# Attention scores of a decoder layer: six bf16 partial products, or three float32r ones in two halves of the array

## The reference, cut to what matters

```python
q = jnp.einsum('oc,bct->bot', Wq, target) + bq[None, :, None]
k = jnp.einsum('oc,bcs->bos', Wk, source) + bk[None, :, None]
v = jnp.einsum('oc,bcs->bos', Wv, source) + bv[None, :, None]
...
dot = jnp.einsum('bhdt,bhds->bhts', q, k) / math.sqrt(HEAD_DIM)
mask = target_mask[:, :, :, None] * source_mask[:, :, None, :]
dot = mask * dot - (1.0 - mask) * NEG
amap = jax.nn.softmax(dot, axis=-1) * mask
out = jnp.einsum('bhts,bhds->bhdt', amap, v)
```

## Time and profile before

| | before |
|---|---|
| median of three runs | 3174.01 us |
| runs | 3170.85 to 3174.55 us |
| span of the profiled execution | 3175.0 us |
| PE, busy | 2991.9 us (94%) |
| DVE, busy | 2833.2 us (89%) |
| ACT, busy | 2419.9 us (76%) |
| POOL, busy | 2094.4 us (66%) |
| bytes moved by DMA | 312.0 MB |

### The profile page before, as it was taken

The page is one execution under the profiler, slowest core; times in us unless marked ns, Lnnn a source line. Parts: engine busy times, 40 slices in busy tenths (PEclk is TensorE's granted clock), DMA queues, the critical chain, the costliest instruction groups (busy, mean ns, idle before and its releaser), DMA issues. The chain is left out here.

```text
span 3175.0 us, 47891 instructions
## 1 busy us (share of the span) xinstructions
PE 2991.9 (94%) x16134; PEld 1833.1 (58%) x16134; DVE 2833.2 (89%) x4149; ACT 2419.9 (76%) x4531; POOL 2094.4 (66%) x1207
## 2 busy tenths in 40 slices
PE   7899999999999999999987699999999999799998
PEld 4777677767776777777755244444444444244444
DVE  6999999999999999999998788888888888288887
ACT  4888888888888888888875177777777777577786
POOL 5999999999999999999998234334334334100000
PEclk9999999999999999999998699999999999899999
DMA  4112211222022202220221656655655653221111
GB/s 176 32 46 81 81 49 43 80 81 69 23 80 81 79 13 80 84 81 15 77 96 64 180 163 178 182 181 174 186 181 171 183 180 113 101 77 47 47 41 37
DMA packets 164389, 311.97 MB, mean 98 GB/s; under 512 B 22736, under 2 KB 80208, under 8 KB 164000
## 3 DMA queue, kind: packets, MB, share of 16 engines
q1 hardware_dynamic: 158784, 299.53, 29.6%
q10 hardware_dynamic: 5360, 9.38, 1.0%
HBM read 217.16 MB, written 91.69 MB: 97 GB/s over the span
## 5 line engine op out<-in xcount | busy, mean ns | idle before, releaser
L830 POOL TENSOR_TENSOR bu<-du,bc 128x1024 f32<-128x1024 f32 x512 | 1199.0, 2370 | 32.1 <-DMA bc<-bc_scratch 29.9
L708 ACT ACTIVATE states<-dt,negA 128x256 f32<-128x256 f32 x2048 | 852.8, 463 | 240.2 <-DVE hc L926 229.4
L914 DVE TENSOR_TENSOR_SCAN states<-states,bu 128x512 f32<-128x512 f32 x704 | 821.5, 1212 | 10.5 <-ACT states L708 8.2
L1568 DVE TENSOR_REDUCE mmax<-s_ps 128x1 f32<-128x512 f32 x1024 | 673.0, 686 | 126.1 <-PE s_ps L1288 105.2
L1413 ACT ACTIVATE pt<-s_ps 128x512 f32<-128x512 f32 x1024 | 579.6, 595 | 209.5 <-PE s_ps L1297 203.7
L926 DVE TENSOR_TENSOR hc<-states,bc 128x512 f32<-128x512 f32 x704 | 445.7, 674 | 1.6 <-DMA bc<-bc_scratch 1.6
L1288 PE MATMUL s_ps<-kst,qst 102*128 102x512 bf16 x1024 | 400.5, 393 | 28.6 <-DMA kst<-mask_d 19.3
L526 PEld LDWEIGHTS y_ps<-id_sb,hc 128*128 128x128 f32 x2816 | 330.7, 143 | 122.9 <-DVE hc L926 58.2
L526 PE MATMUL y_ps<-id_sb,hc 128*128 128x128 f32 x2816 | 377.1, 277 | 22.8 <-DVE hc L926 22.8
L1297 PE MATMUL s_ps<-qst,kst 105*128 105x512 bf16 x1024 | 387.4, 382 | 5.8 <-ACT pt L1413 3.9
L839 POOL TENSOR_TENSOR hp<-hp,bc 128x1024 f32<-128x1024 f32 x160 | 379.5, 2372 | 2.8 <-DVE hp L914 1.9
(11 more groups left out here) (172 smaller groups left out, 4170.6 us busy)
## 6 DMA issues: line engine op xcount, KB each, us to landing
bc<-bc_scratch SPq DMA_DIRECT2D x128, 512.0 KB, 5.2
stack_d<-parts SPq DMA_DIRECT2D x180, 256.0 KB, 3.0
qst<-stack_d SPq DMA_DIRECT2D x64, 384.0 KB
kst<-stack_d SPq DMA_DIRECT2D x64, 384.0 KB
x<-xres SPq DMA_DIRECT2D x31, 512.0 KB, 4.8
w_raw<-in_w_ffn SPq DMA_DIRECT2D x48, 256.0 KB, 2.8
w_raw<-in_w_ffn SPq DMA_DIRECT2D x16, 768.0 KB, 7.3
xT_sb<-in_xT SPq DMA_DIRECT2D x16, 512.0 KB, 6.0
```

The lines of the kernel that those rows point to most:

```text
L708: a = act.activation(states[:, bank, first:first + SEQ], dt[:, t, :], ACT.Exp, scale=negA[:, t, c * NS + n:c * NS + n + 1])
L830: pool.tensor_tensor(bu[:, buf, :].rearrange("p (n l) -> p n l", n=NS), du[:, t % (2 * GRP):t % (2 * GRP) + 1, :].to_broadcast([P, NS, SEQ ...
L914: dve.tensor_tensor_scan(dst, src, bu[:, BU_OF[k][0], cols], 0.0, ALU.mult, ALU.add).then_inc(scan_done, 1)
L1568: dve.tensor_reduce(mmax[:, u // HG, c:c + 1], s1_ps[:, n % S_BANKS], AX.X, ALU.max).then_inc(s1_free, 1)
```

## The change

The scores come from three products of two float32r parts instead of six products of three bf16 parts. The rows of a head are 3 x 16 = 48 (`BLK`), 3 for the masks (`ROWS1` = 51) and 2 for the maximum (`ROWS2` = 53), so that a head fits in 64 partitions. Even heads of the stacks lie in partitions 0 to 63, odd ones in 64 to 127 (`SIDES`, `SIDE`). In a unit `scores_max` takes head u, and `scores_exp` its neighbour in the other half, `other(u)`. `qst` and `kst` keep their bytes: half the heads in the free dimension, four bytes an element.

What goes with it: k and q are split by one cast on ACT and one subtraction on POOL, at units 4 and 8, not two of each (also for the first batch); the maxima by one subtraction; `store_parts` issues 3 DMAs an operand, not 6; `load_group` issues 8 DMAs, not 4, and `max_rows` two copies a group, not one, since each side has its own; the shared products go in two halves behind the second and the fourth pair. The host orders the rows of the weights for q and k to match.

```diff
-PAIRS = ((0, 0), (0, 1), (1, 0), (1, 1), (0, 2), (2, 0))
+PAIRS = ((0, 0), (0, 1), (1, 0))
 BLK = len(PAIRS) * HDIM
 ROWS1 = BLK + len(PAIRS)
-ROWS2 = ROWS1 + 3
-MINUS_ONES = -(1 + 0xBF80 * 2.0 ** -23)
+ROWS2 = ROWS1 + 2
+SIDES = 2
+SIDE = P // SIDES
+GS = HG // SIDES
+LOADS = 2 * 2 * SIDES
+STORES = 2 * len(PAIRS)
...
-        parts = sb("parts", [P, 3, SEQT, HID], BF16)
-        qst = sb("qst", [P, 2, HEADS, HID], BF16)
-        kst = sb("kst", [P, 2, HEADS, HID], BF16)
+        parts = sb("parts", [P, 2, SEQT, HID])
+        qst = sb("qst", [P, 2, HEADS // SIDES, HID])
+        kst = sb("kst", [P, 2, HEADS // SIDES, HID])
...
+        def other(u):
+
+            return u ^ 1
...
-                    sp.dma_start(st[0:BLK, par, g * HG:(g + 1) * HG, :],
-                                 stack_d[opnd, m, :, h0:h0 + HG, :]).then_inc(stack_in[g], 16)
                     src = rows(mask_d, f * 2 + opnd, len(PAIRS) * HID).rearrange("(r o t) -> r o t", t=HID, o=1)
-                    sp.dma_start(st[BLK:ROWS1, par, g * HG:(g + 1) * HG, :],
-                                 src.to_broadcast([len(PAIRS), HG, HID])).then_inc(stack_in[g], 16)
+                    for side in range(SIDES):
+                        first, h1 = side * SIDE, h0 + side * GS
+                        sp.dma_start(st[first:first + BLK, par, g * GS:(g + 1) * GS, :],
+                                     stack_d[opnd, m, :, h1:h1 + GS, :]).then_inc(stack_in[g], 16)
+                        sp.dma_start(st[first + BLK:first + ROWS1, par, g * GS:(g + 1) * GS, :],
+                                     src.to_broadcast([len(PAIRS), GS, HID])).then_inc(stack_in[g], 16)
...
-                    sp.dma_start(qst[ROWS1:ROWS2, par, g * HG:(g + 1) * HG, :].rearrange("p h t -> p (h t)"),
-                                 m_d[g].rearrange("a c t -> a (c t)")).then_inc(m_in[g], 16)
+                    by_side = m_d[g].rearrange("a (j s i) t -> s a j (i t)", s=SIDES, i=TT)
+                    for side in range(SIDES):
+                        first = side * SIDE
+                        sp.dma_start(qst[first + ROWS1:first + ROWS2, par, g * GS:(g + 1) * GS, :], by_side[side]).then_inc(m_in[g], 16)
...
-                pe.matmul(s1_ps[:, n % S_BANKS, :], qst[0:ROWS1, par, u, tt * P:(tt + 1) * P],
-                          kst[0:ROWS1, par, u, :], start=True, stop=True).then_inc(s1_ready, 1)
+                first, slot = u % SIDES * SIDE, u // SIDES
+                pe.matmul(s1_ps[:, n % S_BANKS, :], qst[first:first + ROWS1, par, slot, tt * P:(tt + 1) * P].bitcast(F32R),
+                          kst[first:first + ROWS1, par, slot, :].bitcast(F32R), start=True, stop=True).then_inc(s1_ready, 1)
...
-                pe.matmul(s2_ps[:, n % S_BANKS, :], kst[0:ROWS2, par, u, st * P:(st + 1) * P],
-                          qst[0:ROWS2, par, u, :], start=True, stop=True).then_inc(s2_ready, 1)
+                first, slot = other(u) % SIDES * SIDE, u // SIDES
+                pe.matmul(s2_ps[:, n % S_BANKS, :], kst[first:first + ROWS2, par, slot, st * P:(st + 1) * P].bitcast(F32R),
+                          qst[first:first + ROWS2, par, slot, :].bitcast(F32R), start=True, stop=True).then_inc(s2_ready, 1)
...
-                cuts = [0, len(products) // 4, len(products) * 3 // 4, len(products)]
+                cuts = [0, len(products) // 2, len(products)]
...
-                        if tt == 0:
-                            shared_part(u - 1, 2)
-                        if tt >= 2:
-                            shared_part(u, tt - 2)
+                        if tt == 1 or tt == 3:
+                            shared_part(u, tt // 2)
...
-                if i == 0:
-                    pool.tensor_tensor(x[:, :, :], x[:, :, :], parts[:, 0], ALU.subtract).then_inc(rest[kind], 1)
-                else:
-                    pool.tensor_tensor(parts[:, 2], x[:, :, :], parts[:, 1], ALU.subtract).then_inc(done, 1)
+                pool.wait_ge(cast[kind], batch)
+                pool.tensor_tensor(parts[:, 1].bitcast(F32R), x[:, :, :], parts[:, 0], ALU.subtract).then_inc(done, 1)
```

More of the change, by code:

```diff
@@ L7 @@
 BF16 = mybir.dt.bfloat16
+F32R = mybir.dt.float32r
 ALU = mybir.AluOpType
@@ L746, in last_rows @@
                     scale_first()
-                for (kind, i), at in CAST_AT.items():
+                for kind, at in CAST_AT.items():
                     if at == k:
-                        cast_first(kind, i)
+                        cast_first(kind)
             def measure(b, i):
@@ L803, in _ @@
             for side, part in enumerate((mk, mk_n)):
[L804 to L812, removed]
+                at = [[pair[side] for pair in PAIRS].index(i) for i in range(2)]
                 pool.drain()
                 for r, pair in enumerate(PAIRS):
-                    if r not in at:
-                        pool.tensor_copy(mk_rows[:, side, r, :], mk_rows[:, side, at[pair[side]], :])
+                    if pair[side] == 0:
+                        pool.tensor_copy(mk_rows[:, side, r, :].bitcast(F32R), part)
+                pool.drain()
+                pool.tensor_tensor(mk_rows[:, side, at[1], :].bitcast(F32R), part, mk_rows[:, side, at[0], :], ALU.subtract)
             pool.drain()
@@ L846, in last_rows @@
                     pool.tensor_tensor(a_rs, a_ve, a_half, ALU.pow).then_inc(a_stats, 1)
-                for (kind, i), at in REST_AT.items():
+                for kind, at in REST_AT.items():
                     if at == k:
                         x, parts = a_kf if kind == "k" else a_qf, a_parts[kind]
-                        pool.wait_ge(a_cast[kind], i + 1)
-                        dst = x if i == 0 else parts[:, 2]
-                        pool.tensor_tensor(dst, x, parts[:, i], ALU.subtract).then_inc(a_rest[kind], 1)
+                        pool.wait_ge(a_cast[kind], 1)
+                        pool.tensor_tensor(parts[:, 1].bitcast(F32R), x, parts[:, 0], ALU.subtract).then_inc(a_rest[kind], 1)
             def body(b, par):
@@ L1193, in max_rows @@
                     for g in groups:
-                        wait(m_in[g], b * 16)
+                        wait(m_in[g], b * (SIDES * 16))
                 wait(m_split, seq("m", b, idx))
@@ L1238, in body @@
                         for g in range(HGROUPS):
-                            wait(stack_in[g], f * (4 * 16))
+                            wait(stack_in[g], f * (LOADS * 16))
                     wait(k_split, f)
@@ L1255, in body @@
                 if active(f):
-                    wait(parts_out, f * (12 * 16))
+                    wait(parts_out, f * (STORES * 16))
                 group(0)
@@ L1373, in shared @@
                         m = pe.matmul(dst, lhsT, rhs, start=start, stop=stop)
-                if products and part == 2:
+                if products and part == 1:
                     m.then_inc(mm[kind], 1)
@@ L1412, in exponentials @@
                     act.wait_ge(s2_ready, b * 64 + u * TT + st + 1)
-                    act.activation(pt[:, g % 2, u % HG, st, :], s2_ps[:, score(b, u, st) % S_BANKS], ACT.Exp).then_inc(exp_done, 1)
+                    act.activation(pt[:, g % 2, other(u) % HG, st, :], s2_ps[:, score(b, u, st) % S_BANKS], ACT.Exp).then_inc(exp_done, 1)
             def load_ctx(f, par):
@@ L1425, in _, with round_part @@
             act.dma_start(bv_sb[:, :], bv.partition_broadcast(P)).then_inc(params, 16)
-            def round_part(kind, f, i):
+            def round_part(kind, f):
                 x = kf if kind == "k" else qf
-                if i == 0:
-                    act.wait_ge(ev[kind], seq(kind, f, 1))
-                    if kind == "q":
-                        act.wait_ge(parts_out, (f - 1) * (12 * 16) + 6 * 16)
-                    elif not (isinstance(f, int) and f == 1):
-                        act.wait_ge(parts_out, (f - 1) * (12 * 16))
-                else:
-                    act.wait_ge(rest[kind], f)
-                act.activation(parts[:, i], x[:, :, :], ACT.Copy).then_inc(cast[kind], 1)
+                act.wait_ge(ev[kind], seq(kind, f, 1))
+                if kind == "q":
+                    act.wait_ge(parts_out, (f - 1) * (STORES * 16) + STORES // 2 * 16)
+                elif not (isinstance(f, int) and f == 1):
+                    act.wait_ge(parts_out, (f - 1) * (STORES * 16))
+                act.activation(parts[:, 0].bitcast(F32R), x[:, :, :], ACT.Copy).then_inc(cast[kind], 1)
             def mask_values(s, par, idx):
@@ L1461, in body @@
                     for kind, unit in SPLIT_AT.items():
-                        if u - unit in (0, 1) and active(f):
-                            round_part(kind, f, u - unit)
+                        if u == unit and active(f):
+                            round_part(kind, f)
                     if u % HG == HG - 1:
@@ L1477, in body @@
                                 if not (isinstance(b, int) and b + off == 0):
-                                    act.wait_ge(m_in[g], (b + off) * 16)
```

(7 more changed lines are left out.)

56 lines of the change are left out of this document (24 added, 32 removed).

## The result

The kernel after took 3250.9 us (median of four runs, 3246.1 to 3258.1), the kernel before 3173.7 (3170.9 to 3174.6). The ratio is 1.0246, interval 1.0232 to 1.0261: slower by 77 us, where 3109 was predicted. The profiled execution took 3250.0 us, with a span of 3248.2.

A forecast was written before the change was run, and what follows sets the result against it. PE was taken to bound the attention stage, DVE close behind. Attention gains of 62.5 us plus 3 in the first stage, 65.5 off the 3175.0 span, gave 3109 us; main range 3080 to 3135, wider range to 3185.

The forecast's parts named there:

- the moved shared product: Attention units with shared work: its two halves make five steps of array shape at 0.15 us, 0.75 in all.
- the main case: Whole kernel: f32r at the bf16 rate and halves overlapping give 3109 us, own range 3080 to 3135; chance 0.66.
- a pair costs as one: Attention scores on PE: two f32r products in separate row halves overlap and take 0.218 us; upper bound 0.436.
- The changes of shape: PE in attention units: each step into or out of an array shape costs 0.15 us, from 0.12 to 0.19.
- weight loads not hidden: Rival, score pairs on PE: a load waits for its half's product, a pair takes 0.32 us, 3142 us; chance 0.07.
- DVE's idle time: Attention stage: DVE's wait for scores falls from 5.9 to 1.6 us a batch, winning 4.3.
- the clock falls: Rival, light attention units: PE drops to 1.2 GHz, 1.1 us over DVE in four units, 3172 us; chance 0.04.
- The start of the kernel: Mask rows made before 19 us, POOL then free until 47 us: less work there is worth 0.
- the subtractions of the last batch: First stage's last batch: two POOL subtractions fall away, worth 3 us, bounds 0 and 4.3.
- float32r near the bf16 rate: Score products on PE: one f32r product of 512 columns takes 0.218 us; upper bound 0.86.
- the maxima's copies on time: DMA queue, groups 0 and 1: copies about as near the deadline as before, 0 us; rival late 3155, chance 0.04.
- a pair is no pair: Rival, score pairs: halves run in turn or f32r at half rate, 0.436 a pair, 3243 to 3265 us; chance 0.13.

The follow-up runs named there:

- on PE (3153): The changed kernel with the whole shared product behind the fourth pair, in one portion, not two halves: 3152.8 us, 0.993 of the kernel before.
- on DVE (3176): The changed kernel with DVE emptying `misc` ahead of the unit's first maximum, PE's program untouched: 3175.7 us, 1.0007 of the kernel before.
- evacuation first: The changed kernel with DVE emptying `misc` ahead of the unit's first maximum, shared products still in two halves: 3175.7 us, 1.0007.
- the bf16 views: The changed kernel with score products on bf16 views (high part) of each float32r element, in the same halves: 3213.3 us, one execution.
- the whole-array run: The changed kernel with float32r score products over all 128 partitions, both heads in one contraction, exponentials scaled by 1e-9: 3218.2 us, one execution.
- the best kernel: The changed kernel with the whole shared product in one portion behind the fourth pair: 3152.8 us, 0.993 of the kernel before.
- in one half: The changed kernel with both products of a pair in the same half (`other(u)` returns u): 3336.4 us, one execution.
- the last experiment: The changed kernel with the whole shared product behind the fourth pair, plus dummy POOL work (six 16x512 operations, two 128x1024 subtractions): 3157.4 us, one execution.

## Why the prediction was wrong

**The failed step: the moved shared product.** The prediction counted "two pairs, values, half of the shared work, two pairs, the other half: five steps", and priced the move by its steps of shape alone. It never asked what the moved half waits for. The bank `misc` is shared. The first half now comes a pair earlier, at a time when DVE still has the unit's first maximum ahead of the evacuation. The wait measures 5.7 us a batch on PE, where the sum had nothing. Undoing it from either side, on PE (3153) or on DVE (3176), takes back 98 or 75 us, and the bf16 kernel loses 38 us to the same edit. Neither the main case nor a rival had this wait; the range ended at 3185 because nothing in it could reach 3250 without an array that doesn't overlap. But the wait is only half of the story: with it gone and PE's program unchanged (3176) the kernel is no faster than the one before, and 67 us slower than forecast.

**The term that was too small: a pair.** The sum took each pair at 0.218 us, "a pair costs as one". That holds inside a block (0.23 to 0.24 from the second pair on), but the first pair of each block takes 0.33. A unit whose shared work goes out in two halves has two blocks of two pairs, so half of its pairs are first ones. Without its wait the turn unit shown is 3.75 - 0.61 = 3.14, where 2.92 was in the sum; a projection unit without a wait is 4.44 (2040.69 to 2045.13 with evacuation first), where 4.22 was. Both are 0.22 over, two times 0.11.

The changes of shape were priced about right. In that projection unit the five are 0.14 (values to projection: 1.00 less 0.86), 0.19 twice (projection half to pair: 1.06 less 0.87), 0.11 and 0.10 (the last pair of each block: 0.33 and 0.32 less 0.22), so 0.73 where 0.75 was forecast. That the 0.11 of a first pair isn't shape is what the bf16 views (0.24) and the whole-array run (0.11 with no new shape) show. The rival "weight loads not hidden" had a pair at 0.32 for all pairs; it came true for the first of each block. Over 12 units a batch 0.22 is 2.6 us, by estimate most of the 3.3 by which evacuation first (58.3) stays over the forecast 55.

PE is busy for 401.5 / 7.08 = 56.7 us a batch in after, and its 6.9 us of standing still make up the 63.6.

**DVE's idle time** was to be 1.6 us a batch. It was 10.4 after, and 5.2 even in the best kernel (41.1 / 7.84). In that kernel PE is busy for 55.1 us a batch and idle for 2.3, so it takes 57.4 where 55 was forecast, even once placed well. How much of the 5.2 is bursts and how much the v units was not traced unit by unit.

**The clock in the first iteration.** The rival "the clock falls" was priced for the light units of every batch, and there the clock stayed at 1.00. It fell in the first iteration instead, where the sum had no term: 0.50 against 0.66, and 16 us lost there. With evacuation first the clock is 0.50 there too (1757 to 1820 us), and 10.6 of the 16 us remain.

**The start of the kernel** was priced at 0, because POOL has nothing to do between 19 and 47 us. But DVE's scalings of that time start 0.54 us apart on average while POOL casts and subtracts for the masks, and 0.20 us apart later. After has less POOL work there:

```profile
10.20 2.23 DVE L873 TENSOR_SCALAR diagW<-id_sb,chan_sb 128x128 f32<-128x128 f32 x4
...
12.55 0.86 DVE L873 TENSOR_SCALAR diagW<-id_sb,chan_sb 128x128 f32<-128x128 f32 x4
...
42.51 2.34 POOL L823 TENSOR_TENSOR bu<-du,bc 128x1024 f32<-128x1024 f32 x1 [30.36 <-DMA bc<-bc_scratch]
```

POOL's first `bu` starts at 42.5 instead of 47.2, and POOL bounds that whole phase (444 `bu` from 270 to 1738 us with no idle before them), so the 4.7 us last to its end. With the subtractions of the last batch the gain was 11.7 us, not 3. The 2.7 us between those and 4.7 + 4.3 were not traced.

**What held.** float32r near the bf16 rate, one record for each product; the halves overlap (starts 0.01 us apart, against 0.24 in one half); the price of a change of shape; the clock at 1.00 in the steady part; and the maxima's copies on time: PE waits for none of them in the 450 us. The stores did not get shorter as counted, 6 of them take 18.09 us on SP's queue for 12 of 16.57, but PE doesn't wait for the stacks either. The rival "a pair is no pair" named 3243 to 3265 us and the time fell in it by chance, through another mechanism: in after a pair takes 0.33 or less, and 0.43 is seen only where a pair stands alone.

## What to carry to other kernels

When a change moves an instruction earlier on an engine that works in order, look up what that instruction waits for before counting what it costs: here a shared bank emptied behind another engine's longer task turned a 0.6 us wait into a late score for a second engine. Price every way out of a block of products and back by the round trip (0.37 us here: 0.26 for two changes of shape, 0.11 for the first float32r pair), and group products of one shape and type, but not so far that the engine that consumes them runs dry (2.9 us without a score lost more than the steps saved). And a helper engine's work at the very start can slow its neighbour, even when its own result isn't needed for long.

## What had not been expected of the hardware

In the last experiment a DVE TENSOR_SCALAR of 128x128 f32 that starts 0.06 us after a POOL TENSOR_TENSOR of 16x512 (1.03 us) lasts 1.06 us, to the end of POOL's; the next one, between two operations of POOL, lasts 0.28. This repeats for all six of POOL's operations. A row that merges four of them (2.43 us) looks like a steady 0.6 us each, and is not that. The Trainium skill, SBUF — State Buffer, section Who interferes with whom, has tensor_scalar among the operations that can contend with GpSimd for a shared pair of ports, where the one that comes second is fully blocked for the other's instruction. These rows agree. They don't for POOL's first operation, a TENSOR_SCALAR of 2.00 us (4.90 to 6.90 us): beside it DVE starts an instruction every 0.20 to 0.56 us.

A float32r pair that is the first of a block takes 0.33 us to the next pair, where bf16 in the same place takes 0.24; within a block the float32r products of one half were 0.23 to 0.24 apart.
